# Two norms of a two-stage transformer kernel scaled by ScalarE instead of VectorE, with the bias, the store and load of x and its statistics in later slots

## What is computed

```python
x = x + _L0_attn_a_ref(_layernorm(x), Wq, Wk, Wv, Wpost)   # 16 heads of 64, softmax, gelu
x = x + _L0_ffn_ref(_layernorm(x), W1, b1, W2, b2)         # ternary weights, relu
x = x + _L0_attn_b_ref(_layernorm(x), ...)                 # 16 heads of 16, rotary embedding
x = x + _L0_ffn_ref(_layernorm(x), W1, b1, W2, b2)         # the same ffn again
```

## Time and profile before

| | |
|---|---|
| three runs, median | 3813.62 us (3811.97 to 3814.59) |
| the profiled execution, device time | 3815.57 us |
| its span in the trace | 3813.7 us |
| busy PE, VectorE, ScalarE, GpSimd | 96%, 71%, 61%, 50% |
| PE's granted clock, mean | 0.982 of full speed |
| first scores of stage two (L691) | 2274.5 us |

### The profile page before, as it was taken

How to read it: one execution, slowest core, us unless ns; L and a number is a source line. 1 busy time by engine, 2 the same in 40 slices (tenths; PEclk the granted TensorE clock), 3 DMA queues, 4 the chain that set the end, 5 groups by cost and what they waited for, 6 DMA issues and landing times.

```text
span 3813.7 us, 64079 instructions
## 1 busy us (share of the span) xinstructions
PE 3650.5 (96%) x23938; PEld 2451.6 (64%) x23938; DVE 2720.9 (71%) x4342; ACT 2330.4 (61%) x4501; POOL 1917.1 (50%) x1210
## 2 busy tenths in 40 slices
PE   8999999999999999999999878999999999999987
PEld 5777777777777777777777654555555555555534
DVE  6766666667676666666667667888888888888762
ACT  5665666566566656656656435666666666666654
POOL 4555555545555555555555433555555555555412
PEclk9999999999999999999999988999999999999988
DMA  2000000000000000000000012222222222222220
GB/s 78 7 12 1 12 12 12 1 12 12 1 12 12 7 7 12 12 1 12 12 1 15 25 48 56 52 58 61 59 57 61 58 57 57 57 57 57 51 45 17
DMA packets 86965, 114.16 MB, mean 30 GB/s; under 512 B 6660, under 2 KB 60420, under 8 KB 86660
## 3 DMA queue, kind: packets, MB, share of 16 engines
q1 hardware_dynamic: 86660, 110.07, 11.5%
HBM read 33.43 MB, written 25.17 MB: 15 GB/s over the span
## 4 chain that ended last, share of the span: by engine, by line
PE 84%; DVE 9%; ACT 3%; issue 2%; POOL 2%; DMA 0%; DVEq 0%; POOLq 0%; ACTq 0%
PE ps_o L642 12%; PE ps_s L611 10%; PE ps_t L624 8%; PE ps_t L218 7%; PE ps_o L718 6%; PE ps_t L753 5%; PE ps_s L691 5%; PE ps_m L624 4%; PE ps_t L225 4%; PE ps_t L744 4%; PE ps_m L218 4%; PE ps_t L677 3%; DVE max_b L1114 3%; PE ps_s L705 3%; PE ps_m L744 2%
## 5 line engine op out<-in xcount | busy, mean ns | idle before, releaser
L511 POOL TENSOR_TENSOR e_a<-e_a,recip 128x1024 f32<-128x1024 f32 x512 | 969.4, 1894 | 955.7 <-DVE recip L983 955.6
L796 ACT ACTIVATE e_a<-ps_s,neg_max 128x512 f32<-128x512 f32 x1024 | 694.3, 685 | 548.5 <-DVE neg_max L976 548.2
L1114 DVE TENSOR_REDUCE max_b<-ps_s 128x2 f32<-128x1024 f32 x512 | 623.6, 1219 | 177.7 <-PE ps_s L691 176.0
L838 ACT ACTIVATE et<-ps_s 128x1024 f32<-128x1024 f32 x512 | 523.7, 1023 | 357.1 <-PE ps_s L705 356.8
L976 DVE TENSOR_REDUCE neg_max<-ps_s 128x2 f32<-128x1024 f32 x512 | 622.7, 1216 | 68.7 <-PE ps_s L611 68.7
L642 PE MATMUL ps_o<-et_a,v_a 128*64 128x256 f32 x4096 | 500.2, 386 | 9.6 <-DVE heads_a L1019 5.2
L611 PE MATMUL ps_s<-raw_a 64*128 64x512 f32 x3072 | 426.0, 409 | 8.8 <-ACT e_a L796 8.7
L543 POOL TENSOR_TENSOR h_lo<-h,h_hi 128x512 fp32r<-128x512 f32 x248 | 320.5, 1305 | 183.1 <-ACT h_hi L880 183.1
L642 PEld LDWEIGHTS ps_o<-et_a,v_a 128*64 128x64 f32 x4096 | 279.6, 137 | 192.8 <-issue 79.2
L990 DVE COPY et_a<-ps_t 128x512 f32<-128x512 f32 x366 | 250.9, 687 | 207.0 <-PE ps_t L624 202.8
L624 PE MATMUL ps_t<-ident,e_a 128*128 128x128 f32 x2660 | 395.0, 281 | 2.1 <-DVE xl L1164 2.0
(11 more groups left out here) (196 smaller groups left out, 7315.7 us busy)
## 6 DMA issues: line engine op xcount, KB each, us to landing
q_stack<-roped_q SPq DMA_DIRECT2D x256, 96.0 KB
k_stack<-roped_k SPq DMA_DIRECT2D x256, 96.0 KB
x_a<-X SPq DMA_DIRECT2D x16, 512.0 KB, 3.9
X<-x_a SPq DMA_DIRECT2D x16, 512.0 KB, 2.9
x_ahead<-X SPq DMA_DIRECT2D x16, 512.0 KB, 3.8
X<-x_ahead SPq DMA_DIRECT2D x16, 512.0 KB, 4.9
x_before<-X SPq DMA_DIRECT2D x16, 512.0 KB, 3.8
OUT<-x_before SPq DMA_DIRECT2D x16, 512.0 KB, 5.1
```

What stands on the lines that cost most here:

```text
L511: nc.gpsimd.tensor_tensor(e_a[:, u % 5, :, :], e_a[:, u % 5, :, :], factor, ALU.mult).then_inc(e_normed, 1)
L796: ins = nc.scalar.activation(e_a[:, u % 5, h, :], ps_s[:, 2 * (u % 2) + h, :], ACT.Exp, bias=neg_max[:, u % 5, h:h + 1], accum_out=sums[:, ...
L838: nc.scalar.activation(et[:, v % 5, :, :], ps_s[:, 2:4, :], ACT.Exp)\
L1114: nc.vector.reduce_max(max_b[:, u // 4 % 2, :, u % 4], ps_s[:, score_bank(u):score_bank(u) + 2, :], AX.X, negate=True).then_inc(max_done, 1)
```

## The change

ScalarE scales x for the norms "ffn0" and "attn"; "ffn1" stays with VectorE. ScalarE computes `x * rstd + shift`, where shift is minus the mean times rstd. VectorE writes `minus_mean` in the aggregation (for all three norms), and GpSimd multiplies it with `rstd` after the power, for the two norms. The scaling comes last in ScalarE's step, behind the exponentials.

All five pieces of "ffn0" move to later steps. The first three pieces of "attn" stay, its scaling and its bias move to later steps, and the store of x and the load of the next move with them. Of the file's numbers, only these change.

```diff
--- before.py
+++ after.py
@@ -55,6 +55,8 @@
         ident = at("ident", 0, [P, P])
         rstd = at("rstd", 0.5, [P, TB])
         minus_half = at("minus_half", 0.53125, [P, TB])
+        shift = at("shift", 1.4375, [P, TB])
+        minus_mean = at("minus_mean", 1.46875, [P, TB])
         stats = at("stats", 0.5625, [P, TB, 6])
         mean_var = at("mean_var", 0.6875, [P, TB, 2])
         neg_max = at("neg_max", 0.75, [P, 5, 2])
@@ -164,6 +166,7 @@
         a_rstd_ready = sem("a_rstd_ready")
         rstd_ready = sem("rstd_ready")
         a_xn_ready = sem("a_xn_ready")
+        shift_ready = sem("shift_ready")
         xn_ready = sem("xn_ready")
         a_xh_ready = sem("a_xh_ready")
         xh_ready = sem("xh_ready")
@@ -298,8 +301,8 @@
         QK, VB = (-41.5, -40, -38, -36), (-34, -33.5, -31.6, -31.1)
         WO1, XT1 = (98.5, 100.5, 104.5, 106.5), (118.1, 119.1)
         UP1, DOWN1 = (128, 129, 130.5, 132, 133, 134.5, 136.5, 138.5), (140.5, 142.5, 146.5, 148.5)
-        NORM = {"ffn0": (-108, -106, -105, -103, -98), "attn": (-67, -64, -63, -60, -58), "ffn1": (103, 108, 109, 113, 115)}
-        BIAS = {"ffn0": -88, "attn": -57, "ffn1": 124}
+        NORM = {"ffn0": (-104, -103, -101, -95, -91), "attn": (-67, -64, -63, -51, -49), "ffn1": (103, 108, 109, 113, 115)}
+        BIAS = {"ffn0": -88, "attn": -47, "ffn1": 124}
         ROTATE, HIGHS, LOWS = (-39, -37, -35, -34, -32, -30), (-34, -33, -29, -28), (-31, -30, -28, -26)
         STACK = (-18, -16, -11, -9, 5, 7, 21, 23)
         INVERT, SCALE_HEADS = (42, 58, 74, 90), (46, 62, 76, 92)
@@ -344,6 +347,7 @@
 
         norms = sorted((SLOT * s + NORM[part][0], part, s) for s in range(BATCH) for part in NORM)
         nth_norm = {(part, s): n for n, (_, part, s) in enumerate(norms)}
+        nth_shift = {(part, s): n for n, (_, part, s) in enumerate(norm for norm in norms if norm[1] != "ffn1")}
         norm_steps = {}
         for _, part, s in norms:
             for piece in range(5):
@@ -489,9 +493,9 @@
                     for step in (2 * (slot - SHIFT), 2 * (slot - SHIFT) + 1):
                         for s in range(BATCH):
                             r = step - SLOT * s
-                            if r == -115:
+                            if r == -108:
                                 load_ahead(s)
-                            if r == -54:
+                            if r == -46:
                                 save_ahead(s)
                             if r in STACK:
                                 stack(s, STACK.index(r))
@@ -529,6 +533,9 @@
                 def inverse_deviation(part, s):
                     pool.wait_ge(var_ready, nth_norm[part, s] + 1)
                     nc.gpsimd.tensor_tensor(rstd[:, :], rstd[:, :], minus_half[:, :], ALU.pow).then_inc(rstd_ready, 1)
+                    if part != "ffn1":
+                        pool.wait_ge(rstd_ready, nth_norm[part, s] + 1)
+                        nc.gpsimd.tensor_tensor(shift[:, :], minus_mean[:, :], rstd[:, :], ALU.mult).then_inc(shift_ready, 1)
 
                 def add_bias(part, s):
                     pool.wait_ge(xn_ready, TB * (nth_norm[part, s] + 1))
@@ -838,6 +845,14 @@
                     nc.scalar.activation(et[:, v % 5, :, :], ps_s[:, 2:4, :], ACT.Exp)\
                         .then_inc(exp_done, 1)
 
+                def normalise(part, s, first):
+                    act.wait_ge(shift_ready, nth_shift[part, s] + 1)
+                    if part == "ffn0" and s == 0:
+                        act.wait_ge(a_x_out, 16 * (BATCH - 1))
+                    for t in (first, first + 1):
+                        nc.scalar.activation(xn[:, t, :], x_of[part][:, t, :], ACT.Identity, scale=rstd[:, t:t + 1],
+                                             bias=shift[:, t:t + 1]).then_inc(xn_ready, 1)
+
                 def copy_values(n):
                     act.wait_ge(values_done, 4 * n + 4)
                     if n == 0:
@@ -928,6 +943,9 @@
                                 copy_values(QUADS * s + (r - 40) // 16)
                         if step % 2 == 0 and 0 <= step // 2 - L < UNITS_ALL:
                             exps(step // 2 - L)
+                        for piece, part, s in norm_steps.get(step, []):
+                            if piece > 2 and part != "ffn1":
+                                normalise(part, s, 2 * (piece - 3))
 
             @block.vector
             def _(dve):
@@ -1082,12 +1100,11 @@
                     for t in range(TB):
                         ins = nc.vector.bn_aggr(mean_var[:, t, :], stats[:, t, :])
                     link(ins)
+                    nc.vector.tensor_scalar(minus_mean[:, :], mean_var[:, :, 0], -1.0, None, ALU.mult)
                     nc.vector.tensor_scalar(rstd[:, :], mean_var[:, :, 1], EPS, None, ALU.add).then_inc(var_ready, 1)
 
                 def normalise(part, s, first):
                     dve.wait_ge(rstd_ready, nth_norm[part, s] + 1)
-                    if part == "ffn0" and s == 0:
-                        dve.wait_ge(a_x_out, 16 * (BATCH - 1))
                     for t in (first, first + 1):
                         nc.vector.tensor_scalar(xn[:, t, :], x_of[part][:, t, :], mean_var[:, t, 0:1], rstd[:, t:t + 1],
                                                 ALU.subtract, ALU.mult).then_inc(xn_ready, 1)
@@ -1209,7 +1226,7 @@
                                 statistics(part, s, 2 * piece)
                             elif piece == 2:
                                 aggregate(part, s)
-                            else:
+                            elif part == "ffn1":
                                 normalise(part, s, 2 * (piece - 3))
                         for s in range(BATCH):
                             r = step - SLOT * s

```

## The result

The changed kernel took 3822.44 us (median of 19 runs, 3819.77 to 3826.26) and the kernel before 3814.68 (19 runs beside them, 3809.81 to 3821.44). The ratio is 1.0019 with a 95% interval of 1.0012 to 1.0026: **slower by 7.8 us**. The profiled execution took 3819.80 us, 4.2 more than the one before, with a span of 3818.0. It lies at the lower edge of its runs, so the trace accounts for 4 of the 8 us. I call it a fall when the granted clock of PE (its share of full speed, PEclk) drops from 1.00 to about half, that is from 2.4 to 1.2 GHz, for a while.

The account below looks back on a forecast made before the run. It took TensorE to bound the second stage, busy 90.09 of each steady 93.60 us. Terms -3.6 - 3.5 - 1.9 - 1.2 + 6.5 = -3.7 us, applied to 3813.62, gave 3810 us; own range 3802 to 3821, with rivals 3797 to 3832.

Parts of the forecast that it names:

- The rotation slides and PE issues L705 0.8 us later: Steady intervals: power and shift inside GpSimd's rotation delay its end 0.81 us and PE's L705 after the exponentials, +0.8 us.
- the activation: ScalarE's 128x256 normalisation: taken as 0.50 us each, costing nothing in slot 18 unless it takes over 0.9 us.
- the shift: GpSimd's 32 small products after the power: taken as 0.25 us each, with 1.02 us as upper bound.
- The bias no longer collides, the stall before slot 21 vanishes, -0.9: Steady intervals: GpSimd's bias waits for ScalarE's last pair, missing VectorE's key subtraction; PE's 0.86 us stall goes, interval -0.1 us.
- the subtraction ends with the bias: VectorE's L1110 beside GpSimd's bias: the later instruction waits for all of the other, 2.62 us beside 0.68.
- the slower rival: Steady intervals: rotation fully late, bias meets the keys' second L1110, 0.86 us stall stays; +17 us, 3830 us, chance 0.27.
- The rival's clock term, +10: Within the slower rival: clock losses over the steady intervals cost 10 us, beside +1.3 us in each of twelve.
- The clock, +6.5 us: Steady intervals: PE's clock falls in about half of them, 5 more at 1.3 us each, +6.5 us (bounds 0 and 15).
- The first two intervals, -3.6 us: First two second-stage intervals: without VectorE's L1092 on PE's uncovered path, -3.6 us together (bounds -1 and -6).
- The 2.68 us of the chain: Slot 15 of the first interval: an L1092 pair in the wait chain, over half covered by PE's work, 1.2 us gained.
- Before the first scores and at the end of stage one, -5.4: VectorE freed of L1092: -3.5 us before the first scores, -1.9 us at the end of stage one.
- Store and load of x: nothing: Second stage: x arrives about two slots, 6 us, after the old statistics' place, in time for the new ones; no cost.

Follow-up runs that it names:

- late_copy: The changed kernel with ScalarE's copy of the last key half one step later, behind slot 18's exponentials; 1.0106 of the kernel before.
- between: The changed kernel with most steps of both norms three earlier, ffn0's pairs on ScalarE staying in slots 16 and 18; 1.0068 of the kernel before.
- Engine alone: The changed kernel with every step back where the kernel before had it, ScalarE still scaling both norms; 1.0079 of the kernel before.
- positions alone: The kernel before, all scaling on VectorE and no shift, with every step at the change's place; 1.0146 of the kernel before.
- ffn0_only: The changed kernel with only ffn0 scaled by ScalarE (slots 16 and 18), attn by VectorE, other steps as before; 3804.27 us, 0.9966 of the kernel before.
- bias_waits: The kernel before with one wait added: GpSimd's ffn0 bias waits for VectorE's last subtractions for queries and keys; 0.9962 of the kernel before.

## Why the prediction was wrong, point by point

The forecast was 3810 us, -3.7; the kernel moved by +7.8. The slide of the rotation and the end of the collision came as written. The steps that failed are two terms of the sum: the number of clock falls (five more at +6.5 us; seven more intervals and 11.6 us measured) and the gain in the first two intervals (-3.6 us; +0.9 measured).

- **The rotation slides and PE issues L705 0.8 us later.** Right: +0.78 by the rows. The wait before slot 18 was 0.49 (forecast 0.55), the activation 0.59 us (taken 0.50, still below the 0.9 from which it would count), the shift 0.20 (taken 0.25).
- **The bias no longer collides, the stall before slot 21 vanishes, -0.9.** Right in kind. At most 0.27 us is left of 0.86. The steady interval at full clock was to be 0.1 us shorter and is equal. I had written that the subtraction ends with the bias; by rows 4 and 7 it ended 0.55 us after it. The stake was also right: `late_copy` shows what the bias costs if it does start ahead of the subtraction, which is the condition of the slower rival; the change misses it by 0.6 us. The rival's clock term, +10, was nearer than mine.
- **The clock, +6.5 us: the term that failed most.** I forecast five more falls at 1.3 us. The price was right for most (1.2 to 1.4); but there were seven more intervals with a fall, one of which cost 2.9 us, and the term measures 12.8 - 1.2 = 11.6 us. My estimate "in about half the intervals" came from a stall of 1.3 us preceded by one of 0.55; the stalls were 1.39 and 0.49, and three of four intervals had a fall. No row carried that estimate, and the runs give no rule in its place: the waits of `between` are larger and as close, and brought no fall.
- **The first two intervals, -3.6 us: did not come.** They took 0.9 us more (167.5 against 166.6). I had counted L1092 where it lay on the path, and one wait there did shrink: that of 0.98 us for maxima in slot 4 became 0.34. But I had not carried the slide into these intervals, which have a rotation as well: in slots 18 and 19 of the first, PE now waits 1.08, 1.20 and 1.10 us, where it waited 0.73 and 1.19. The 2.68 us of the chain brought no more than the wait of 0.48 us before slot 17, which is gone; the longest wait, 2.82 us before slot 11, is 2.81 now. All in all PE's idle time in the two intervals fell by only 0.4 us, and its busy time rose by 1.3, in the first interval, where the clock was 0.83 instead of 0.85.
- **Before the first scores and at the end of stage one, -5.4.** Right in size, -5.8. The reason, VectorE's relief, is only part of it. Kernels that scale on VectorE at the steps of before have their first scores at 2273.5 to 2276.3. Engine alone, on ScalarE at the same steps, has them at 2270.8; positions alone, where VectorE scales everything, at 2270.2. So either half brings most of the gain, and kernels that are alike up to that point differ by up to 2.8 us there.
- **Store and load of x: nothing.** Right; VectorE never waited for them in the steady part.
- **What I had not priced:** -2.9 us in the interval after the steady part, where PE's clock had been 0.92 in the kernel before and is 1.00 now. It is luck of the two profiled executions, as shown above, and it hides as much of the loss.
- **The range.** Half of each distance to a bound, added up, gives 3801 to 3826, not 3802 to 3821; the rest of the sum stands as I worked it.

Put together, with what was measured: -5.8 + 0.9 + 11.6 - 2.9 + 0.5 = +4.3 us, the difference of the two spans. The other 3.5 us up to the medians are not settled in a trace. Of them 2.6 are the distance of the changed kernel's median run from its profiled one. Its runs follow the clock: those of 3819.8 to 3820.1 us have a mean granted clock of 0.981, the median run 0.980, those above 3824 us 0.978 to 0.979. That points to more falls in them; where they stand no trace shows.

## What to carry to other kernels

The same sum of waits on TensorE can cost more in one order than in another: read the granted clock behind each stall and price a fall as its own term, from a pair of intervals with and without one. Take the number of falls from a run; the lengths and distances of the waits did not tell it here. A few matmuls that nothing reads, sized from the trace to be shorter than the stall, measure in one run what the clock costs. And where a late instruction collides with another engine's long one, an explicit wait is cheaper than a fortunate order: one such wait took 0.4% off here.

## What the runs showed of the hardware

Added work on PE made a kernel faster: three matmuls of filler per interval took the ratio from 1.0019 to 0.9984, through the granted clock alone. It fell in nine of twelve intervals behind waits of 0.49 and 1.39 us, in none of six behind waits of 0.85 and 1.41 us equally far apart, in two and four of twelve where the longest wait was a single one of 1.25 to 1.26 us (`ffn0_only`, `bias_waits`), and in none of the steady intervals of the eight runs without a wait over 0.9 us there. A subtraction of two operands on VectorE beside GpSimd's bias took 2.73 us in place of 0.67, four times longer for a start 0.19 us behind the bias: that is why tenths in the order decide whole microseconds of this kernel.
